# Three stages of a graph layer, each moved further behind the sums that feed it: at 3, 6 and 9 groups in place of 1, 2 and 4

## What is computed

```
msg  = concat(h[src], h[dst]) @ Mw.T + Mb
s1, s2, mx, mn = sum, sum of squares, maximum, minimum of msg over the arcs into a node
var  = relu(s2/deg - (s1/deg)**2);  std = sqrt(var)
agg  = concat(mx, mn, std, var)
u    = concat(h, agg, agg*logd/4, agg*4/logd) @ Uw.T + Ub
u    = batch-normalised over the nodes
h    = elu(layernorm(leaky_relu(u @ mix_w.T + mix_b) + h))
```

## Time and profile before

| | us |
|---|---|
| median of 3 runs | 2186.88 (2179.98 to 2197.56) |
| the profiled execution | 2167.94 |
| its span | 2166.1 |
| PE busy | 1219.2 |
| GpSimd busy | 1286.6 |
| DVE busy | 710.3 |
| ACT busy | 313.7 |

### The profile page before, as it was taken

How to read it: one execution, slowest core, us unless ns; L and a number is a source line. 1 busy time by engine, 2 the same in 40 slices (tenths; PEclk the granted TensorE clock), 3 DMA queues, 4 the chain that set the end, 5 groups by cost and what they waited for, 6 DMA issues and landing times.

```text
span 2166.1 us, 14665 instructions
## 1 busy us (share of the span) xinstructions
PE 1219.2 (56%) x4692; PEld 874.3 (40%) x4692; DVE 710.3 (33%) x1711; ACT 313.7 (14%) x807; POOL 1286.6 (59%) x1344
## 2 busy tenths in 40 slices
PE   6520675655546683175575637485156556646585
PEld 5310453444434452153453525353145344434452
DVE  8800423333222352042232413253033223223344
ACT  0110410110000144010100100035011000000015
POOL 2756477666766406666666666604757767667604
PEclk9995788777777796587786868697578878678798
DMA  6253233333333213323233333203323333233300
GB/s 61 70 147 92 59 97 92 89 87 94 98 84 92 61 46 115 92 85 95 88 94 94 87 95 92 86 27 116 104 73 93 94 89 96 86 92 95 92 10 30
DMA packets 88488, 183.62 MB, mean 85 GB/s; under 512 B 31790, under 2 KB 47489, under 8 KB 88409
## 3 DMA queue, kind: packets, MB, share of 16 engines
q0 software_dynamic: 61264, 164.22, 26.8%
q1 hardware_dynamic: 27150, 18.51, 3.9%
HBM read 169.06 MB, written 14.98 MB: 85 GB/s over the span
## 4 chain that ended last, share of the span: by engine, by line
another core or an unknown queue 46%; PE 28%; issue 12%; ACT 7%; DVE 5%; POOL 1%; DMA 0%; SPq 0%; DVEq 0%; ACTq 0%; POOLq 0%
PE ps L689 12%; PE ps L712 7%; PE ps L699 2%; ACT base L830 1%; PE ps L709 1%; PE ps L674 1%; PE ps L754 1%; PE ps L639 1%; PE ps L719 1%; PE ps L739 1%; ACT msq L846 1%; ACT u_sb L863 1%; ACT agg L850 0%; ACT base L828 0%
## 5 line engine op out<-in xcount | busy, mean ns | idle before, releaser
L548 POOL DMA_INDIRECT G<-p_by_rank,index x812 | 796.0, 980 | 525.6 <-issue 227.4
L689 PE MATMUL ps<-G,wide_ident 128*128 128x256 f32 x2436 | 634.6, 410 | 19.8 <-DMA G<-p_by_rank,index 12.2
L689 PEld LDWEIGHTS ps<-G,wide_ident 128*128 128x128 f32 x2436 | 499.5, 209 | 122.1 <-issue 17.5
L548 POOL DMA_INDIRECT G<-p_by_node,index x406 | 399.7, 985 | 217.5 <-issue 129.3
L712 PE MATMUL ps<-w_u_sb,aggT 128*128 128x384 f32 x600 | 266.6, 598 | 217.8 <-issue 137.0
L1261 DVE SCALAR_TENSOR_TENSOR u_sb<-ps,amp,u_sb 128x128 f32<-128x128 f32 x75 | 26.3, 351 | 824.4 <-ACT u_sb L863 599.7
L712 PEld LDWEIGHTS ps<-w_u_sb,aggT 128*128 128x128 f32 x600 | 137.9, 236 | 341.8 <-issue 200.8
L699 PE MATMUL ps<-wide_ident,agg 128*128 128x128 f32 x300 | 61.3, 339 | 339.8 <-ACT agg L850 254.2
L699 PEld LDWEIGHTS ps<-wide_ident,agg 128*128 128x128 f32 x300 | 42.2, 171 | 364.3 <-ACT agg L850 268.7
L719 PE MATMUL ps<-wide_ident,u_sb 128*128 128x128 f32 x75 | 23.8, 318 | 181.9 <-DVE u_sb L1263 101.2
L1140 DVE TENSOR_TENSOR acc<-G 128x512 f32<-128x512 f32 x150 | 96.4, 684 | 39.7 <-DMA G<-p_by_rank,index 38.5
(11 more groups left out here) (202 smaller groups left out, 1158.0 us busy)
## 6 DMA issues: line engine op xcount, KB each, us to landing
G<-p_by_rank,index POOLq DMA_INDIRECT x812
G<-p_by_node,index POOLq DMA_INDIRECT x406
p_by_rank<-base SPq DMA_DIRECT2D x12, 512.0 KB, 3.0
p_by_node<-G SPq DMA_DIRECT2D x6, 514.0 KB
w_u_sb<-in_w_u SPq DMA_DIRECT2D x3, 768.0 KB
x_r<-rows_by_rank SPq DMA_DIRECT2D x1, 1600.0 KB
windows<-src_pad SPq DMA_DIRECT2D x1, 1118.0 KB, 25.1
index<-rows_by_rank SPq DMA_DIRECT2D x1, 468.0 KB
```

Of the source, the lines that this page charges most:

```text
L548: g.indirect_dma_start(G[:, n % R, j, 0:w], None, table, bass.IndirectOffsetOnAxis(ap=index[:, t, k0 + j:k0 + j + 1], axis=0))\
L689: ins = mm(out_ps, ident[:, :], G[:, n % R, k, 0:2 * D], start=False, stop=n in END and k == nk - 1)
```

## The change

The distances at which the stages stand behind a tile's last group are named, and made longer. The positions of the engines' shares of the work in the steps follow from them.

```
+    TURN, UPDATE, TURN_UPDATE = 3, 6, 9
 PE, stage_a:
-                for n in range(NG + 5):
+                for n in range(NG + TURN_UPDATE + 1):
-                    if n - 4 in END:
-                        turn_update(l, END[n - 4])
-                    if n - 2 in END:
-                        update(l, END[n - 2])
-                    if n - 1 in END:
-                        turn(l, END[n - 1])
+                    if n - TURN_UPDATE in END:
+                        turn_update(l, END[n - TURN_UPDATE])
+                    if n - UPDATE in END:
+                        update(l, END[n - UPDATE])
+                    if n - TURN in END:
+                        turn(l, END[n - TURN])
 ACT, stage_a:
-                    if n - 4 in END:
-                        copy_update(l, END[n - 4])
-                    if n - 2 in END:
-                        copy_product(l, END[n - 2])
-                    if n - 1 in END:
-                        deviation(l, END[n - 1])
-                        copy_turned(l, END[n - 1])
+                    if n - TURN_UPDATE - 1 in END:
+                        copy_update(l, END[n - TURN_UPDATE - 1])
+                    if n - UPDATE - 1 in END:
+                        copy_product(l, END[n - UPDATE - 1])
+                    if n - TURN - 1 in END:
+                        copy_turned(l, END[n - TURN - 1])
+                    if n - TURN + 1 in END:
+                        deviation(l, END[n - TURN + 1])
 DVE, stage_a:
-                    if n - 6 in END:
-                        statistics(l, END[n - 6])
-                    if n - 4 in END:
-                        combine(l, END[n - 4])
-                    if n - 1 in END:
-                        variance(l, END[n - 1])
+                    if n - TURN + 1 in END:
+                        variance(l, END[n - TURN + 1])
+                    if n - UPDATE - 1 in END:
+                        combine(l, END[n - UPDATE - 1])
+                    if n - TURN_UPDATE - 2 in END:
+                        statistics(l, END[n - TURN_UPDATE - 2])
```

More of the change, by code:

```diff
@@ L872, in stage_a @@
                 bases(l)
-                for n in range(NG + 5):
-                    if n - 4 in END:
-                        copy_update(l, END[n - 4])
-                    if n - 2 in END:
-                        copy_product(l, END[n - 2])
-                    if n - 1 in END:
-                        deviation(l, END[n - 1])
-                        copy_turned(l, END[n - 1])
+                for n in range(NG + TURN_UPDATE + 2):
+                    if n - TURN_UPDATE - 1 in END:
[6 more added lines that the diff above has]
+                        deviation(l, END[n - TURN + 1])
                     if l == 0 and n < NG:
@@ L1276, in stage_a @@
                 dve.sem_inc(extras_done.sem, 1)
-                for n in range(NG + 7):
-                    if n - 6 in END:
-                        statistics(l, END[n - 6])
-                    if n - 4 in END:
-                        combine(l, END[n - 4])
-                    if n - 1 in END:
-                        variance(l, END[n - 1])
+                for n in range(NG + TURN_UPDATE + 3):
+                    if n - TURN + 1 in END:
[4 more added lines that the diff above has]
+                        statistics(l, END[n - TURN_UPDATE - 2])
                     if n == 2 and l < L - 1:
```

## The result

| | before | after |
|---|---|---|
| median of the runs, us | 2188.59 (2179.98 to 2197.56, 4 runs) | 2216.74 (2209.12 to 2218.09, 4 runs) |
| span of the profiled execution, us | 2166.1 | 2207.4 |
| idle of GpSimd between a layer's gathers beyond 0.30 each, three layers, us | 201.6 | 228.7 |
| of it, pauses over 1 us | 47 | 41 |
| last sums behind the last gather, three layers, us | 99.0 | 107.5 |

The ratio is 1.0128, with a 95% interval of 1.0089 to 1.0167: the change makes the kernel slower by 1.3%, where 3% faster was forecast. The rows of idle and of distances are summed from the records of all 406 gathers of each layer. They hold the first filling of the ring, and pauses that the view of waits puts to "issue", so they are larger than the prediction's 153.5.

What follows compares the result with a forecast made beforehand. PE's late signals while gathers run were taken to bound the kernel, making GpSimd pause at the ring. Savings 40 + 16 + 10 - 1 = 65 us from 2168 gave 2103, plus 19: 2122, rounded to 2120; range 2015 to 2198.

Steps and rivals of the forecast that it cites:

- prediction's 153.5: GpSimd's waits for the ring over three layers, less the 0.30 us of pace in each: 153.5 us.
- What bounds the kernel: While gathers run, PE's signals reach readers tens of us late; GpSimd uses up the ring and pauses some 4 us.
- ACT and DVE. I cost this at nothing: Copies and combine one step behind PE's stages: signals come in order, 16 groups of ring cover it; 0 us.
- DVE in step with PE: Rival: combine ahead of compare waits for update, holding DVE and GpSimd; 56 us slower, 2243; chance 0.15.
- The sign I had named as the one against me: Prediction would be wrong if DVE's `dve_used` became what GpSimd waits for.
- Pauses fall by 26%, 40 us: PE's stages at 3, 6, 9: progress per cycle rises from 7 to 9.5 groups, saving 40 of 153.5 us.
- rival of no change: Running on only queues work up, or signals come at a rate of their own; time stays 2187; chance 0.18.
- The first form of that rival: PE really works slowly in the gaps, hidden by the records; running on only queues work; time stays 2187.
- The backlog, -16: At a layer's end PE stands 2.5 groups nearer to GpSimd, at 2.1 us each, three layers: 16 us saved.
- The first cycle, -10: Start of second and third layer: PE takes groups 4 to 6 before needing a late signal; 5 us a layer saved.
- The end, +1: Last tile's chain gets `turn_update` and `copy_update` of the tile before in front: some 0.4 us a layer, 1 us lost.
- All of it goes, 1949: Rival: pauses and backlog both vanish, 153.5 + 85 = 238 us, giving 1949 us; chance 0.15 for anything under 2060.

Runs made afterwards that it cites:

- g: Kernel before with each gather replaced by a plain DMA of 128 consecutive rows, issued from GpSimd's queue: 1217 us.
- h: Kernel before with each gather replaced by a plain DMA of 128 consecutive rows, issued from SP's hardware queue: 1214 us.
- m: Kernel before with GpSimd held to 8 groups ahead in the ring of 16, on a chip of 1886 us: ratio 1.0003.
- k: Changed kernel with DVE's combine two steps behind update, as in the kernel before, in place of one: 0.9937 of the kernel before.
- a: Changed kernel with DVE's compare moved ahead of variance and combine in a step: 0.9983 of the kernel before.
- l: Changed kernel with compare first on DVE and two gathered rows in one matmul of 512 columns: 2161.23 us, 0.9873 of the kernel before.
- e: Kernel before with PE summing only every other gathered row of a group: 2143 us, ratio 0.9875.
- f: Kernel before with the squares left out, PE summing 128 of the 256 columns of each row: 2163 us, ratio 0.9954.
- i: Kernel before with indirect gathers of the second and third layer fetching 512 bytes a row in place of 1024: ratio 1.0022.
- j: Kernel before with a ring of 12 slots in place of 16: ratio 0.9907.
- o: Changed kernel with a ring of 12 slots, on a chip of 1886 us: 1.0005 of the kernel before.
- p: Changed kernel with compare first on DVE, two rows in one matmul and 12 slots, on a chip of 1886 us: 0.9988 of the kernel before.
- d: Kernel before with two gathered rows in one matmul of 512 columns, halves added at a tile's end: 2158 us, ratio 0.9953.

## Why the prediction was wrong

**What bounds the kernel: right, with a limit.** Late signals of PE held GpSimd at the ring, and they are a matter of gathers under way: with plain transfers (g, h) they are gone, and on the chips of 1886 us too, and there with them the pauses (none over 1 us in m) and most of the backlog (12.4 us in m). The limit is that this is no property of the kernel. No view of one profile could show that another chip doesn't have it.

**"ACT and DVE. I cost this at nothing": the step that failed.** I argued that an engine held by an early signal misses no later one, and that 16 groups cover the rest. Both are true up to the moment that matters. When the late signals come out together, GpSimd needs the slots at once, and the cover has been used up; that is why it stands. DVE then has `combine` and one or two compares to do before its `dve_used`. This takes 2.2 to 3.3 us in 13 pauses, between 20 and 37.9 us in all, and GpSimd's idle time grew by 27. It is the mechanism of the rival, to which I gave 0.15: "DVE in step with PE". Its price was half of the tiles at 1.5 us, 56 us; it was 13 of 75 tiles at up to 2.9 us, and the median rose by 28. The sign I had named as the one against me, `dve_used` as what GpSimd waits for, is what the profile shows. The reason that I set against it, that PE's signal is as late for GpSimd as for DVE, is where the argument broke: equal lateness puts DVE's work behind the signal, not beside it. What k shows limits this: the time came back there while most of DVE's waits stayed (80 of 96 us), so how much of the loss lay in these pauses isn't settled. That the loss goes when DVE's order is changed is shown by a and k together, each with one thing moved on DVE.

**"Pauses fall by 26%, 40 us": failed too, and a shows it apart from DVE.** The pauses did become fewer, 47 to 41, 13%; in a 39, in l 34. But I took them to last 4 us each whatever their number, and their sum is what stays: 201.6 us in before, 207.4 in a and 206.8 in l. It stays with half of PE's sums (e), half their columns (f) and half of the bytes (i), within 193 and 215. By layer there are 14, 13 and 14 pauses, where 10 to 13 were to be seen. The sentence in the rival of no change, "if signals come out at a rate of their own whatever PE has done, result and time are the same as here", describes this best. It had a chance of 0.18. The first form of that rival, PE slowly at work in the gaps and a longer run-on that only fills its queue, is not ruled out either: the last section has 63 instructions waiting and one done in 1.40 us. My reason against it, signals that come together, did not weigh enough. With DVE out of the way, no change is what was measured. That PE's run-on sets the number of pauses I had taken from the numbers of pauses alone, with no row in which the run-on differed.

**The backlog, -16: it was +8.5,** at 35.7, 34.6 and 37.2 us a layer where 20 to 27 were to be seen. A full ring at the last gather sets most of its length: j shows 36 us less for four slots and three layers. In a and k, with 16 slots, it is 79.0 and 83.4 us, which one profile each does not explain.

**The first cycle, -10: nothing.** The first three pauses of the second layer were 10.4, 2.8 and 2.3 us, and are 11.6, 5.2 and 5.9; so 7 us more; in the third layer their sum is 15.7 and 15.5.

**The end, +1: it was +8.5,** and not for `turn_update` of the tile before, which I had priced, but for its `combine`, which stands ahead of the last tile's `close` on DVE, and for the lower clock of the update behind PE's wait.

**All of it goes, 1949:** no change to the order did that, but the chips of 1886 us show what it would be, and the bound of 153.5 + 85 = 238 us was too low by some 50. Between the spans of before, 2166.1, and of m, 1881.0, lie 195 us in the three stretches of gathers, 84 behind them and 7 ahead of the first layer. The 195 hold the first filling of the ring, which I had left out as 27 us.

## What to carry to other kernels

When a step with a long wait is put off, look at what it stands in front of on its own engine at its new place. If a shared ring is used up whenever late signals come out, the work between the signal and the release of the slot can be paid, however idle that engine is. If the sum of a stall stays while PE's work, the bytes and the ring are changed, an order is unlikely to cure it; take the suspect out in a run before costing a cure. Repeat the kernel before on another chip before trusting such a stall. And where the producer always ends with the ring full, a deeper ring is a longer backlog: 12 slots were faster than 16 where signals were late (j), and no slower where they were not (o, p).

## What the runs showed of the hardware

**PE with 63 instructions outstanding.** In the gathers of the kernel after, PE's sums and their weight loads stand alternately and mostly 1.40 us apart from 869 to 912 us (start, duration, idle time ahead):

```profile
870.43 0.38 PE L690 MATMUL ps<-G,wide_ident 128*128 128x256 f32 x1 [2.42 <-issue]
873.23 0.59 PE L690 MATMUL ps<-G,wide_ident 128*128 128x256 f32 x1 [2.42 <-issue]
876.03 0.59 PE L690 MATMUL ps<-G,wide_ident 128*128 128x256 f32 x1 [2.21 <-issue]
```

```profile
871.84 0.19 PEld L690 LDWEIGHTS ps<-G,wide_ident 128*128 128x128 f32 x1 [2.50 <-issue]
874.63 0.29 PEld L690 LDWEIGHTS ps<-G,wide_ident 128*128 128x128 f32 x1 [2.60 <-issue]
```

There are 222 such distances in the three layers, and none in before; of 0.7 us there are 264 and 13. I set PE's recorded semaphore updates (302 of the 333 of the sums are there) beside the records that raise them. Three of them come at 882.32, 893.52 and 915.92 us, 8 and 16 instructions apart, which is 1.40 us for each. Where the steps begin, 63 instructions of PE have started by the records and not yet raised their signal, and there are never more; in before the most is 57, and in m, where signals are in time, 6. The reading that fits both is that a record shows when an instruction is taken in, and that with the queue full the records show the pace at which PE gets done, one in 1.40 or 0.70 us. By this a longer run-on ends at the queue. A full queue is not what kept the gain away: l, with half the sums' records, has 53 such distances in place of 486 and the same sum of pauses, and in d, too, which has the same sum, no more than 41 instructions are outstanding. The Trainium skill (TensorE: Matmul & The Clock Gate, Architectural detail: the array is 16× 32×32, not 1× 128×128) gives TensorE's queue a depth of 64; the 63 agree with it.

**The same gathers, two kinds of chip.** In all profiles from the chips of 2170 to 2189 us PE's signals were late while indirect gathers flowed, up to 35 us in the earlier trace rows, and on the two chips of 1886 us they were in time, with the gathers at 0.98 us each everywhere. The bytes kept coming where signals were late: 105 GB/s in the very stretch in which nothing of PE was recorded. What holds PE up there, and why a sum of some 60 us of pauses in each layer (80 in the first, with the first filling) lets it through, is not settled. It is not the bytes (i) nor their rate (g, h), not GpSimd's software queue by itself (g), and the sum of the pauses does not follow PE's work (d, e, f).
